# Second attention of a two-layer block: null key and value folded in at eviction, products in 64x64 quadrants, one fixed order of ticks

## What is computed

```python
q = _split_heads(jnp.einsum('bnd,df->bnf', x, Wq))
kv = jnp.einsum('bmc,cf->bmf', context, Wkv)
k, v = jnp.split(kv, 2, axis=-1)
k, v = (_split_heads(k), _split_heads(v))
nk = jnp.broadcast_to(null_kv[0], (b, HEADS, 1, DH))
nv = jnp.broadcast_to(null_kv[1], (b, HEADS, 1, DH))
k = jnp.concatenate((nk, k), axis=-2)
v = jnp.concatenate((nv, v), axis=-2)
q = q * scale
sim = jnp.einsum('bhid,bhjd->bhij', q, k)
attn = jax.nn.softmax(sim, axis=-1)
out = jnp.einsum('bhij,bhjd->bhid', attn, v)
out = out.transpose(0, 2, 1, 3).reshape(b, -1, INNER)
out = jnp.einsum('bnf,fd->bnd', out, Wout)
```

## Time and profile before

| | |
|---|---|
| median of 3 runs | 1669.17 us (1668.22 to 1670.46) |
| profiled execution: its own time | 1669.32 us |
| its span | 1667.0 us |
| second attention | 705.5 to 1257.8 us of the span |
| TensorE busy in the span | 1377.0 us (83%) |
| VectorE, ScalarE, GpSimd busy | 1096.7, 942.1, 602.0 us |

### The profile page before, as it was taken

The page is one execution under the profiler, slowest core; times in us unless marked ns, Lnnn a source line. Parts: engine busy times, 40 slices in busy tenths (PEclk is TensorE's granted clock), DMA queues, the critical chain, the costliest instruction groups (busy, mean ns, idle before and its releaser), DMA issues. The chain is left out here.

```text
span 1667.0 us, 36532 instructions
## 1 busy us (share of the span) xinstructions
PE 1377.0 (83%) x13193; PEld 1123.7 (67%) x13193; DVE 1096.7 (66%) x2274; ACT 942.1 (57%) x1676; POOL 602.0 (36%) x664
## 2 busy tenths in 40 slices
PE   4888885799999999759999999999982775877880
PEld 4777773587777787548888888888881663655550
DVE  5888885667777667547667667676666763645552
ACT  4778785665665665445555555555542553655550
POOL 2322220355555556533122122122110763255552
PEclk9999997799999999969999999999995777999995
DMA  4222221322212222130000000000002211145535
GB/s 142 82 96 80 92 89 56 120 81 71 67 49 76 83 70 79 26 97 2 14 14 2 14 15 2 14 15 2 1 2 63 83 50 47 49 137 159 163 130 169
DMA packets 91916, 108.50 MB, mean 65 GB/s; under 512 B 19327, under 2 KB 56703, under 8 KB 91779
## 3 DMA queue, kind: packets, MB, share of 16 engines
q1 hardware_dynamic: 82466, 80.68, 16.2%
q0 software_dynamic: 9312, 26.03, 4.5%
HBM read 61.06 MB, written 29.82 MB: 55 GB/s over the span
## 5 line engine op out<-in xcount | busy, mean ns | idle before, releaser
L827 POOL TENSOR_TENSOR b_h_lo<-b_h,b_h_hi 128x512 fp32r<-128x512 f32 x168 | 216.5, 1293 | 179.0 <-ACT b_h_hi L851 178.5
L1227 POOL TENSOR_TENSOR c_prob<-c_prob,c_recip 128x520 f32<-128x520 f32 x64 | 67.9, 1067 | 401.8 <-DVE c_recip L1517 401.8
L846 ACT ACTIVATE b_zg<-b_zg 128x512 f32<-128x512 f32 x168 | 97.6, 581 | 81.6 <-PE b_zg L890 81.4
L851 ACT ACTIVATE b_h_hi<-b_h 128x512 fp32r<-128x512 f32 x168 | 105.1, 626 | 65.7 <-DVE b_h L1055 65.6
L1907 POOL DMA_INDIRECT planes_dram<-d_y_out,d_back x92 | 93.7, 1019 | 123.3 <-DVE d_y_out L2215 101.4
L1055 DVE TENSOR_TENSOR b_h<-b_zg,b_uw 128x512 f32<-128x512 f32 x168 | 116.2, 691 | 32.0 <-ACT b_zg L846 26.7
L1048 DVE TENSOR_TENSOR b_uw<-b_zu,b_gw 128x512 f32<-128x512 f32 x128 | 88.2, 689 | 57.3 <-PE b_zu L890 50.9
L2184 DVE TENSOR_TENSOR d_h_lo<-d_h,d_h_hi 128x512 fp32r<-128x512 f32 x124 | 81.4, 685 | 29.1 <-ACT d_h_hi L1945 19.2
L1945 ACT ACTIVATE d_h_hi<-d_h 128x512 fp32r<-128x512 f32 x124 | 77.3, 624 | 40.1 <-DVE d_h L2178 40.0
L1270 ACT ACTIVATE c_probT<-c_s 128x1024 f32<-128x1024 f32 x64 | 65.6, 1025 | 51.0 <-PE c_s L1417 50.6
L328 POOL TENSOR_TENSOR a_qx<-a_qT,headmask 128x256 f32<-128x256 f32 x64 | 37.9, 613 | 147.2 <-ACT a_qT L363 147.2
(11 more groups left out here) (357 smaller groups left out, 4248.8 us busy)
## 6 DMA issues: line engine op xcount, KB each, us to landing
rows_dram<-a_blank SPq DMA_DIRECT2D x32, 520.0 KB, 3.2
b_gw<-gates_dram SPq DMA_DIRECT2D x64, 256.0 KB, 3.9
d_up_slot<-d_up_tab POOLq DMA_DIRECT2D x15, 512.0 KB, 3.0
d_down_slot<-d_down_tab POOLq DMA_DIRECT2D x15, 512.0 KB
d_xg<-rows_dram SPq DMA_DIRECT2D x23, 260.0 KB
b_gm<-gates_dram SPq DMA_DIRECT2D x32, 160.0 KB, 3.9
c_craw<-in_c_ctxT_dram SPq DMA_DIRECT2D x8, 512.0 KB, 4.0
d_pay<-planes_dram SPq DMA_DIRECT2D x16, 256.0 KB, 4.5
```

What stands on the lines that cost most here:

```text
L827: pool.tensor_tensor(h_lo[:, m % HS, :], h[:, m % HF, :], h_hi[:, m % HS, :].bitcast(F32), ALU.subtract).then_inc(lo_done.sem, 1)
L846: act.activation(zg_ps[:, n % ZG, :], zg_ps[:, n % ZG, :], ACT.Silu).then_inc(sg_done.sem, 1)
L851: act.activation(h_hi[:, m % HS, :], h[:, m % HF, :], ACT.Copy).then_inc(hi_done.sem, 1)
```

## The change

`attention1` is written anew.

- The null key is subtracted from the keys as ScalarE evicts them (`less_nk` as bias) and the null value from the values as VectorE evicts them. The null score is then zero: the maximum is clipped at zero (`clip`), the null probability is `exp(-top)` (`null_prob`), and it is added to the sum (`add_null`). The null value times Wout is a row `y_null`, made once ahead of the first output product and added when y is read.
- Scores and probabilities have 64 columns a head. Both batch rows of a unit go through one maximum, one subtraction, one exponential, one sum. The probabilities of a pair of heads for both batch rows fill one 128x128 tile, so `turn_probs` turns eight tiles a unit, in two halves of four.
- `scores` and `values` are products of 64 rows by 64 columns in all four quadrants of the array.
- Queries and keys are made for pairs of units (256 columns), half of the head pairs in each tick; values still per unit.
- The output product is three products of 128 columns per head pair.
- x is normalised by ScalarE, the values are evicted by VectorE alone, queries and keys by ScalarE alone, and y is scaled by GpSimd.
- Every engine runs through `ticks` in one order, each function with its own lag. `Tally` is a semaphore with a credit of 8, so that early waits pass.

The diff, cut to what the prediction speaks of; the old functions are in the listing above.

```diff
+        PAIR = 2 * P
...
-        wo = sb("wo", [P, 2, PAIRS, C], F32R)
+        wo_hi, wo_lo = split("wo", [P, PAIRS, C])
...
+        xn = sb("xn", [P, 4, C])
+        x_hi, x_lo = split("x", [P, 2, PAIR])
...
+        s_ps = ps("s", [P, 2, PAIRS, N])
+        t_ps = ps("t", [P, PAIRS, P])
+        oy_ps = ps("oy", [P, 2, 512])
+        o_ps = oy_ps[:, :, 0:256].rearrange("p b (r q) -> p b r q", q=N)
+        xT_ps = oy_ps[:, 0, 256:512].rearrange("p (n t) -> p n t", n=2)
+        y_ps = oy_ps[:, 1, 256:512].rearrange("p (n f) -> p n f", n=2)
...
+        split_at = {-4: (0, WK), -3: (WK, WV), -2: (WV, len(jobs))}
...
+            def scale_y(w):
+                if is_unit(w) and w % GROUP == GROUP - 1:
+                    g = w // GROUP
+                    y = y_sb[:, g % 2, :, :]
+                    wide = lambda t: t[:, :].unsqueeze(1).to_broadcast([P, GROUP, C])
+                    pool.wait_ge(loaded, 16 * len(small))
+                    pool.wait_ge(y_normed.sem, y_normed.at(g + 1))
+                    pool.tensor_tensor(y, y, wide(ln_w), ALU.mult).then_inc(y_scaled.sem, 1)
+                    pool.wait_ge(y_scaled.sem, y_scaled.at(2 * g + 1))
+                    pool.tensor_tensor(y, y, wide(ln_b), ALU.add).then_inc(y_scaled.sem, 1)
+
+            for n in ticks:
+                scale_y(n - 7)
+                scale(n - 1, 0)
+                scale(n - 1, 1)
+                split_context(n + 4)
+                if n in split_at:
+                    weights.rest(pool, *split_at[n], True)
...
+            def keys_out(u, i):
...
+                    act.wait_ge(negated, 1)
+                    act.activation(kx[:, p % 2, r:r + 2, :].rearrange("p r t -> p (r t)"), p_ps[:, i, :], ACT.Identity,
+                                   bias=less_nk[:, 0:1]).then_inc(k_out.sem, 1)
+
+            def null_prob(w):
+                if is_unit(w):
+                    act.wait_ge(clipped.sem, clipped.at(w + 1))
+                    act.wait_ge(added.sem, added.at(w - 1))
+                    act.activation(p0[:, w % 2, :, :], top[:, w % 2, :, :], ACT.Exp, scale=-1.0).then_inc(p0_done.sem, 1)
...
+            for n in ticks:
+                out_upper(n - 1, 0)
+                queries_out(n + 1, 0)
+                roots(n - 3)
+                queries_out(n + 1, 1)
+                keys_out(n + 1, 0)
+                out_upper(n - 1, 1)
+                exps(n + 1)
+                normalise(n + 5)
+                keys_out(n + 1, 1)
+                null_prob(n + 1)
+                x_upper(n + 5)
+                if n in split_at:
+                    weights.scalar(act, *split_at[n])
+                probs_out(n, 0)
+                probs_out(n, 1)
+
 
...
+            def queries(u, i):
...
+                    for n in range(2):
+                        m = three(p_ps[:, i, n * PAIR:(n + 1) * PAIR], wq_hi[:, r0 + n, :], wq_lo[:, r0 + n, :],
+                                  x_hi[:, p % 2, :], x_lo[:, p % 2, :])
+                    m.then_inc(q_made.sem, 1)
+
...
+                    for r in range(PAIRS):
+                        for b in range(2):
+                            for par in range(2):
+                                rows, at = head_rows[par], w % 2 * P + b * N
+                                m = pe.matmul(s_ps[head_rows[par ^ b], b, r, :], qx[rows, p % 2, r, at:at + N],
+                                              kx[rows, p % 2, r, at:at + N], start=True, stop=True)
+                    m.then_inc(scored.sem, 1)
+
+            def turn_probs(w, i):
+                if is_unit(w):
+                    pe.wait_ge(scaled.sem, scaled.at(2 * w + i + 1))
+                    pe.wait_ge(probT_out.sem, probT_out.at(2 * (w - 1) + i + 1))
+                    for r in range(i * QUADS, (i + 1) * QUADS):
+                        m = pe.transpose(t_ps[:, r, :], prob[:, w % 2, r, :, :].rearrange("p b k -> p (b k)"), ident[:, :])
+                    m.then_inc(turned[i].sem, 1)
...
+            def values(w, i):
+                if is_unit(w):
+                    pe.wait_ge(probT_out.sem, probT_out.at(2 * w + i + 1))
+                    pe.wait_ge(v_out.sem, v_out.at(2 * w + i + 1))
+                    pe.wait_ge(lo_o.sem, lo_o.at(2 * w + i))
...
+                        r = i * QUADS + n
+                        for b in range(2):
+                            for par in range(2):
+                                h, at = 2 * r + par, (par ^ b) * N
+                                m = pe.matmul(o_ps[head_rows[par], b, n, :], v[head_rows[b], w % 3, h * D1:(h + 1) * D1],
+                                              probT[head_rows[b], w % 2, r, at:at + N], start=True, stop=True)
...
+            def project(w):
+                if is_unit(w):
...
+                            m = three(y_ps[:, 1, :], nv_hi[:, :], nv_lo[:, :], wo_hi[:, r, :], wo_lo[:, r, :],
+                                      r == 0, r == PAIRS - 1)
+                        m.then_inc(null_made, 1)
+                        pe.wait_ge(null_out, 1)
+                    pe.wait_ge(lo_o.sem, lo_o.at(min(2 * (w + 1) + 1, LAST_Q)))
+                    pe.wait_ge(y_read.sem, y_read.at(w))
+                    rows = lambda t, r: t[:, w % 2, r, :, :].rearrange("p b q -> p (b q)")
+                    for r in range(PAIRS):
+                        m = three(y_ps[:, w % 2, :], rows(oT_hi, r), rows(oT_lo, r), wo_hi[:, r, :], wo_lo[:, r, :],
+                                  r == 0, r == PAIRS - 1)
+                    m.then_inc(projected.sem, 1)
+
+            for n in ticks:
+                values(n - 2, 0)
+                scores(n)
+                queries(n, 0)
+                project(n - 3)
+                queries(n, 1)
+                keys(n, 0)
+                values(n - 2, 1)
+                turn_probs(n - 1, 1)
+                keys(n, 1)
+                values_in(n, 0)
+                turn_x(n + 4)
+                turn_probs(n - 1, 0)
+                values_in(n, 1)
...
+            def values_out(u, i):
+                if is_v(u):
+                    w = u + 1
+                    dve.wait_ge(v_made.sem, v_made.at(v_count(u, i)))
+                    dve.wait_ge(valued.sem, valued.at(2 * (w - 3) + i + 1))
+                    dve.tensor_tensor(v[:, w % 3, i * 512:(i + 1) * 512].rearrange("p (h d) -> p h d", d=D1),
+                                      p_ps[:, i, :].rearrange("p (h d) -> p h d", d=D1),
+                                      nv[:, :].unsqueeze(1).to_broadcast([P, PAIRS, D1]), ALU.subtract).then_inc(v_out.sem, 1)
...
+            def clip(w):
+                if is_unit(w):
+                    dve.wait_ge(topped.sem, topped.at(w + 1))
+                    dve.wait_ge(p0_done.sem, p0_done.at(w - 1))
+                    dve.tensor_scalar(top[:, w % 2, :, :], top[:, w % 2, :, :], 0.0, None, ALU.max).then_inc(clipped.sem, 1)
...
+            def subtract(w):
+                if is_unit(w):
+                    dve.wait_ge(clipped.sem, clipped.at(w + 1))
+                    dve.wait_ge(turned[0].sem, turned[0].at(w - 1))
+                    dve.wait_ge(turned[1].sem, turned[1].at(w - 1))
+                    dve.tensor_tensor(prob[:, w % 2, :, :, :].rearrange("p r b k -> p b r k"), s_ps[:, :, :, :],
+                                      top[:, w % 2, :, :].rearrange("p r b -> p b r").unsqueeze(3).to_broadcast([P, 2, PAIRS, N]),
+                                      ALU.subtract).then_inc(subbed.sem, 1)
...
+            def read_y(w):
+                if is_unit(w):
...
+                    dve.wait_ge(projected.sem, projected.at(w + 1))
+                    dve.wait_ge(added_up.sem, added_up.at(g - 1))
+                    dve.tensor_tensor(y_sb[:, g % 2, j, :], y_ps[:, w % 2, :], y_null[:, :], ALU.add).then_inc(y_read.sem, 1)
+                    dve.wait_ge(y_read.sem, y_read.at(w + 1))
...
+            for n in ticks:
+                read_y(n - 3)
+                clip(n)
+                subtract(n)
+                out_lower(n - 2, 1)
+                add_up(n - 6)
+                normalise_y(n - 4)
+                sums(n)
+                x_lower(n + 4)
+                if n in split_at:
+                    weights.rest(dve, *split_at[n], False)
+                values_out(n, 0)
+                next_stats(n - 7)
+                add_null(n)
+                invert(n)
+                values_out(n, 1)
+                out_lower(n - 1, 0)
+                tops(n + 1)
```

685 lines of the change are left out of this document (263 added, 422 removed).

## The result

The changed kernel takes **1599.47 us** (median of 4 runs, 1596.25 to 1600.99), the kernel before in the same session 1668.7 us (4 runs, 1666.07 to 1670.46): ratio 0.9584, 95% interval 0.9564 to 0.9603, **69.2 us less**. The forecast was 1593 us (76 less), range 1573 to 1655. The profiled execution took 1600.99 us, its span is 1599.2 us, 67.8 less than before.

What follows compares the result with a forecast made beforehand. TensorE's queue was taken to bound the second attention: 32 units x 13.5 us + 44 us of edges = 476 us against 552, -76 us from 1669.2, so 1593 us, range 1573 to 1655.

Steps and rivals of the forecast that it cites:

- The bound: Second attention, steady part: TensorE's own queue sets the pace, 16.10 us per unit before, 13.5 after.
- rival 2: Second attention's ticks: VectorE's `read_y` ring or two thin margins make TensorE wait; 1 us a tick gives 1625 us; chance 0.09.
- The small products: Scores and values on TensorE: four 64x64 tiles side by side, 15 ns a record, 3.8 us a unit becomes 1.9.
- Rival 1: Scores and values: quadrants do not all run side by side, 29 ns a record stays; 1652 us, scores alone 1623; chance 0.18.
- Rival 3: Small products: switching or quadrant loads block others, slower than before above about 34 ns a record, up to 1772 us; chance 0.05.
- 0.8 for edges and waits: TensorE's tick: changes of kind and waits take 1.7 us a unit before, edges 0.9 us after.
- Transposes, values' projection, output product: TensorE per unit: transposes 1.8 us to 0.9, values' projection 2.7 in both, output product 1.9 to 2.7.
- Queries and keys: TensorE's projections: 36 products of 256 columns at 120 ns, 4.3 us a unit, against 4.1 before; bounds 112 and 227 ns.
- The edges: Second attention outside its 32 steady units: 37 us before, 44 us after.
- the null row: Start of the second attention: the null row's product takes 2.7 us.
- the tail: End of the second attention: 8 us, from 6.6 after the last product plus y's two slower passes on GpSimd.
- Ramp and drain: Second attention's ends: 10 us lost in the ramp to weight splits, 1.2 GHz clock and unoverlapped softmax; 7 in the drain.

Runs made afterwards that it cites:

- The filled run: Identity transposes nobody reads put into TensorE's idle time at both ends, against the version with 256-column output product and eight staging slots: 1553.97 us, ratio 0.9374.

## Why the prediction held, point by point

- **The bound, and rival 2.** TensorE's queue sets the pace: doubling the transposes moves the tick by 0.96 us, adding some 1.2 us to VectorE moves it by 0.07. No wait on VectorE or GpSimd stands before TensorE in the steady part.
- **The small products (15 ns, 1.9 us a unit).** 16 ns. Four quadrants instead of two are the largest part that a run takes back, 43 us. Rival 1 is out: four quadrants in a two-by-two arrangement run side by side, as four in a row or in a column did in the earlier trace rows, and the scores are no slower than the values although their two row halves write into the same part of `c_s`. The rule quoted from the Trainium skill (TensorE: Matmul & The Clock Gate, Back-to-back issue gap), no closer than about 25 ns, does not hold here: the scores' records lie 16 ns apart, in loads and in matmuls (951.39 to 952.44 for 64). Rival 3 fell with it.
- **What no run takes back.** The tick fell by 2.91 us. Two quadrants would give 1.33 of it back, doubled transposes 0.84, and the old output product takes another 0.84 off (averages of four ticks). That leaves some 1.6 us a tick, 50 us over 32, to what the change did at once and no run undid: longer batches, the new order, fewer waits. In TensorE's queue, from the start of each block to that of the next, scores and values, waits included, took 4.7 us a unit before and take 2.2 now, and the transposes with x's 2.5 and 1.1; both fell by more than the prices of the prediction say. Its 1.9 us for the small products and its 0.8 for edges and waits nearly came out in the sum, but how they divide is read from the traces and not tried.
- **Transposes, values' projection, output product.** 4 transposes load in 0.42 us, 512 columns stay at 227 ns, 128 columns at 110 to 111: as priced.
- **Queries and keys (120 ns).** 113 ns: taken as the rest of a pair, it was 7 ns too dear, 36 x 0.007 = 0.25 us of the 0.3 by which the tick came out shorter (13.19 for 13.5). The measured price is the prediction's lower bound: 256 columns cost what 128 do. The shorter tick makes −10 us over 32 units.
- **The edges (44 us): the step that failed.** 484.6 − 32 x 13.19 = **62.5 us**, +18. The first product came 16.9 us after the start (16.5 predicted), the null row took 3.2 (2.7), the tail 7.5 (8). Ramp and drain were predicted at 17 us together and took 35. Some 21 of that is the drain, predicted at 7: 38.0 us from the last scores (1145.7) to the end of the last output product, for four output products, five halves of values, 16 transposes and the scores themselves, 17 us at the prices above. The other 14 are the ramp, predicted at 10. So the drain is the term that was mis-sized, by 14 of the 18 us. The ramp's term left out that a weight's DMA holds ScalarE's queue, the eviction behind it and TensorE behind that (4.20 us, then products at half the clock until 741). The drain's term took TensorE's work and not the chain. In the last ticks values, ScalarE's upper half, VectorE's lower half, output product, `read_y` and the other half of the values follow each other, since they share `c_oy`:

```profile
1169.91 0.47 PE L1355 MATMUL c_oy<-c_wo_hi,c_oT_hi 128*128 128x128 f32 x1 [1.44 <-DVE c_oT_lo L1554]
...
1175.76 1.14 PE L1445 MATMUL c_oy<-c_probT,c_v 64*64 64x64 f32 x32 [0.47 <-DVE c_y_sb L1572]
1178.33 0.48 PE L1355 MATMUL c_oy<-c_wo_hi,c_oT_hi 128*128 128x128 f32 x1 [1.43 <-DVE c_oT_lo L1554]
...
1183.30 0.41 PE L1357 MATMUL c_oy<-c_wo_hi,c_oT_lo 128*128 128x128 f32 x1
```

  While TensorE waits, its clock falls to 1.2 GHz, and the last output product takes 5.0 us (1178.33 to 1183.30) where one in the middle takes 2.5. The filled run shows that, with the 256-column product, 6 us of the drain are the clock alone. That the rest is the chain is read from the waits above, and the run with the doubled sum lengthened it by 4 us through VectorE; no run shortened the chain itself.
- **The sum.** −10 for the tick and +18 for the edges make the stage 8.6 us longer than the 476 forecast, and the kernel 6.5 us slower than 1593. Two errors of opposite sign: the total came out closer than its parts, and that is luck.

## What to carry to other kernels

Small products pay by their order as much as by their shape: let each stand behind one of another quadrant, and look at the distance of the weight loads to see whether they run side by side. When a stage of fixed ticks is priced, price its first and last ticks as chains, with the clock that TensorE has after a pause, not as work; here that was worth 18 us, 14 of them in the drain. And before a row of waits is taken as time to be won, look whether TensorE's own products leave a gap there that a plain change of kind would leave as well.

## What the runs showed of the hardware

- The same 64 records of 64x64 cost 16, 29 or 51 ns each, with four, two or one quadrant in turn. Inside a run of one quadrant a record costs 59 ns, and around the join with the next quadrant's run six or seven records start in 0.2 us: a record of another quadrant can start before the run ahead of it is done. How far ahead that reaches was not measured.
- An fp32r product of 256 columns follows the last after 113 ns, one of 128 after 110, one of 512 after 227: between 128 and 256 columns the width costs next to nothing, which is why the product in 256 columns took 24 us off.
- Matmuls whose result nobody reads kept the granted clock at 1.00 through a drain in which it had been 0.68, and the same chain became 6 us shorter. At the start, 40 of them brought the clock from 0.50 to 1.00, and behind the pause of 5.4 us it was at 0.50 again.
